# One softmax guard per head and image as the exp's bias operand, and small TensorE pieces in the even quads

## What is computed

```
h   = patches @ W + b + pos                              # 16 x 1024 x 64
xn  = ln(h)
q, k, v = xn @ Wq + bq, xn @ Wk + bk, xn @ Wv + bv       # 8 heads of 8
scores[b,h,i,j] = q_i . k_j / sqrt(8) + col_bias[h, j]   # 1024 x 1024 per head and image
out = softmax_j(scores) @ v
h   = h + out @ Wo + bo
h   = h + moe(ln(h))      # adds its own input too; experts w1, gelu, w2, 8 of them, top 2
```

## Time and profile before

| | us |
|---|---|
| median of 3 runs | 1176.74 (1175.11 to 1177.24) |
| the profiled execution | 1175.44 |
| its span, first to last instruction | 1173.6 |
| TensorE busy (share) | 1105.3 (94%) |
| ScalarE busy | 1030.7 (88%) |
| VectorE busy | 671.2 (57%) |
| GpSimd busy | 131.8 (11%) |

### The profile page before, as it was taken

One profiled execution on the slowest core, in us unless ns is written; L12 is line 12 of the kernel. 1 busy time (PEld: TensorE's weight loads), 2 busy tenths in 40 slices (PEclk: granted clock), 3 DMA queues, 4 the chain that ended last, 5 costly groups with the idle time before them and its releaser, 6 DMA issues. The chain is left out here.

```text
span 1173.6 us, 21907 instructions
## 1 busy us (share of the span) xinstructions
PE 1105.3 (94%) x7938; PEld 326.1 (28%) x7938; DVE 671.2 (57%) x1899; ACT 1030.7 (88%) x1127; POOL 131.8 (11%) x137
## 2 busy tenths in 40 slices
PE   3399999999999999999999999999999999899998
PEld 3122222222222222222222222222222222233332
DVE  9542756565656555565656565656565624367665
ACT  0199999999999999999999999999999999754553
POOL 4302201010101010101010101010101100000000
PEclk8589999999999999999999999999999999999999
DMA  2421323232323232323232323222222220022332
GB/s 52 111 74 39 85 53 82 53 83 53 83 53 84 53 83 53 83 49 87 49 88 49 86 50 73 63 68 67 62 67 55 72 61 10 16 63 66 84 75 50
DMA packets 63041, 75.93 MB, mean 65 GB/s; under 512 B 26338, under 2 KB 31458, under 8 KB 62906
## 3 DMA queue, kind: packets, MB, share of 16 engines
q1 hardware_dynamic: 60076, 73.01, 25.1%
q10 hardware_dynamic: 2350, 1.10, 0.4%
q0 software_dynamic: 480, 0.06, 0.1%
HBM read 37.54 MB, written 36.49 MB: 63 GB/s over the span
## 5 line engine op out<-in xcount | busy, mean ns | idle before, releaser
L1247 ACT ACTIVATE probs<-psum 128x1024 f32<-128x1024 f32 x1024 | 946.5, 1144 | 13.2 <-PE psum L1446 10.9
L1462 PE MATMUL psum<-probs,VA 128*32 128x512 f32 x4096 | 547.0, 606 | 5.3 <-DVE oT L1315 0.9
L1446 PE MATMUL psum<-QA,KA 54*128 54x512 bf16 x2048 | 331.7, 385 | 20.0 <-ACTq L1266 9.1
L1446 PEld LDWEIGHTS psum<-QA,KA 54*128 54x128 bf16 x2048 | 75.0, 93 | 491.5 <-ACT probs L1247 448.3
L1315 DVE STREAM_TRANSPOSE oT<-psum 128x512 f32<-128x512 f32 x64 | 45.9, 717 | 143.3 <-PE psum L1462 143.3
L1462 PEld LDWEIGHTS psum<-probs,VA 128*32 128x32 f32 x4096 | 82.1, 108 | 144.6 <-issue 86.1
L1282 ACT ACTIVATE probs<-psum,b 128x1024 f32<-128x1024 f32 x64 | 67.9, 1111 | 53.6 <-PE psum L1515 53.5
L1393 DVE TENSOR_TENSOR probs<-probs,psum 128x1024 f32<-128x1024 f32 x64 | 78.2, 1221 | 51.6 <-PE psum L1525 30.4
L484 DVE TENSOR_SCALAR qk<-psum,b_qk,scale_qk 128x512 f32<-128x512 f32 x32 | 25.8, 810 | 134.4 <-PE psum L673 134.4
L1515 PE MATMUL psum<-m_x,w 64*128 64x512 f32 x256 | 60.5, 591 | 1.5 <-ACT probs L1282 1.5
L1539 PE MATMUL psum<-probs,w 128*64 128x512 f32 x256 | 60.9, 598 | 0.0
(11 more groups left out here) (175 smaller groups left out, 830.9 us busy)
## 6 DMA issues: line engine op xcount, KB each, us to landing
QA<-q_parts_d SPq DMA_DIRECT2D x64, 192.0 KB
KA<-k_parts_d SPq DMA_DIRECT2D x64, 192.0 KB
q_parts_d<-qk_parts SPq DMA_DIRECT2D x31, 192.0 KB, 2.5
k_parts_d<-qk_parts SPq DMA_DIRECT2D x31, 192.0 KB, 2.7
xT<-in_xT SPq DMA_DIRECT2D x16, 256.0 KB, 2.6
x_d<-x2T SPq DMA_DIRECT2D x16, 256.0 KB, 2.1
m_x<-x_d SPq DMA_DIRECT2D x16, 256.0 KB, 2.7
out_h<-result SPq DMA_DIRECT2D x16, 256.0 KB, 3.2
```

The source lines that it names most:

```text
L1247: nc.scalar.activation(probs[:, k % PROB_BUFS, :], score_buf(buf_of(k)), ACT.Exp).then_inc(exped, 1)
L1446: last = pe.matmul(score_buf(buf_of(k))[:, (g % 2) * BANK:(g % 2 + 1) * BANK], KA[rows_of(h, SCORE_ROWS), h // 2, jt * P:(jt + 1) * P], QA ...
L1462: last = pe.matmul(o_acc[32 * g:32 * g + 32, :], VA[:, jt, h, :], probs[:, k % PROB_BUFS, (g % 2) * BANK:(g % 2 + 1) * BANK], start=(jt == ...
```

## The change

- The exp of a block gets a bias operand, `lift`, one value per partition: minus the larger bound of the block's two heads. `lift` is made once per image.
- The shift per query is gone, and with it `shift_of`, the DRAM tensor `shift_d` and `store_shift`. The three shift rows of `QA` stay (the fallback writes to them) and are loaded with zeros from SBUF.
- The largest key bias is taken off the bias rows in the prologue.
- A step `bound` takes the place of `flag`: TensorE spreads the 8 bounds to all partitions (ones times a diagonal), VectorE reduces them to `lift` and compares the largest with 31.
- `AUX_SLOTS`: nearly all pieces move to even slots (`bound` is in 15), and VectorE's own slots and `ROUTER_EXP_BLOCK` move along.
- On GpSimd `prep_rstd` of image b+2 moves ahead of `copy_v(0)`; in the prologue `prep_rq` moves ahead of `prep_rstd`.

The diff, cut to its core:

```diff
-AUX_SLOTS = {0: ("qk0", 0), 1: ("qk0", 1), 2: ("qk1", 0), 4: ("qk1", 1), 6: ("out_proj", 0), 7: ("out_proj", 1),
-             10: ("sq", 0), 13: ("post_t", 0), 16: ("router", 0), 18: ("router", 1), 19: ("flag", 0), 20: ("v", 0),
-             21: ("v", 1), 23: ("embed", 0), 24: ("embed", 1), 26: ("combine_t", 0), 29: ("norm_t", 0)}
+AUX_SLOTS = {0: ("qk0", 0), 2: ("qk0", 1), 4: ("qk1", 0), 6: ("qk1", 1), 8: ("out_proj", 0), 10: ("out_proj", 1),
+             12: ("sq", 0), 14: ("post_t", 0), 15: ("bound", 0), 16: ("router", 0), 18: ("router", 1), 20: ("embed", 0),
+             22: ("embed", 1), 24: ("v", 0), 26: ("v", 1), 28: ("combine_t", 0), 30: ("norm_t", 0)}
...
-CENTRE_SLOT, SCALE_SLOT, LEAD_SLOT, NORM_SLOT = 7, 9, 25, 27
-ROUTER_EXP_BLOCK = 38
+CENTRE_SLOT, SCALE_SLOT, LEAD_SLOT, NORM_SLOT = 10, 12, 23, 26
+ROUTER_EXP_BLOCK = 40
...
-COMBINE_SLOT, WEIGH_SLOT = 20, 22
+COMBINE_SLOT, WEIGH_SLOT = 20, 25
...
-                    rows = shift_d.rearrange("a (h t) i -> t a h i", t=2)
-                    sp.dma_start(QA[r, pairs, :], rows[par, :, pairs, :]).then_inc(aug_loaded[hg], 16)
+                    zeros = zeros3[:, :].bitcast(BF16).unsqueeze(1).broadcast_to([PARTS, 2, T])
+                    sp.dma_start(QA[r, pairs, :], zeros).then_inc(aug_loaded[hg], 16)
...
                 elif step == "sq":
-                    v.tensor_copy(sq[:, :], bank)
                     v.reduce_max(sq_max[:, :], bank, AX.X).then_inc(free, 1)
                     v.wait_ge(free, freed)
                     alone(v)
                     square_bounds(link)
-                    shift_of(bp, link, close)
+                    v.wait_ge(rq_ready, bp + 1)
+                    link(v.tensor_scalar(rq_clipped[:, :], rq[:, :], RQ_CLIP, None, ALU.min))
+                    close()
+                    v.tensor_scalar(rq_diag[:, :], ident[0:H, 0:H], rq_clipped[:, 0:1], None,
+                                    ALU.mult).then_inc(rq_spread, 1)
+                elif step == "bound":
+                    v.tensor_reduce(rq_top[:, :], bank[0:1, 0:H], AX.X, ALU.max)
+                    v.tensor_reduce(lift[:, bp % 2, :], bank[:, 0:H].rearrange("p (j t) -> p j t", t=2), AX.X, ALU.max,
+                                    negate=True).then_inc(free, 1)
                     v.wait_ge(free, freed)
...
+                    v.tensor_scalar(flags[0:1, ds(bp, 1)], rq_top[:, :], RQ_LIMIT, None,
+                                    ALU.is_gt).then_inc(flag_ready, 1)
...
+                elif step == "bound":
+                    pe.wait_ge(rq_spread, n + 1)
                     alone(pe)
-                    last = pe.matmul(aux[0:1, 0:1], excess[:, :], ones8[:, :], start=True, stop=True)
+                    last = pe.matmul(aux[:, 0:H], ones8[:, :], rq_diag[:, :], start=True, stop=True)
...
+                    sp.wait_ge(ones_ready, 2)
+                    load_shift(0)
+                    load_shift(1)
...
+                    v.memset(zeros3[:, :], 0.0).then_inc(ones_ready, 1)
...
-                    v.tensor_reduce(bias_top[:, :], bias_hj[:, :, :], AX.X, ALU.max).then_inc(bias_ready, 1)
+                    link(v.tensor_reduce(bias_top[:, :], bias_hj[:, :, :], AX.X, ALU.max))
+                    v.tensor_copy(bias_tops[:, :, :], bias_top[:, :].unsqueeze(2).broadcast_to([P, H, NCH])
+                                  ).then_inc(bias_ready, 1)
...
-                    link(v.tensor_copy(bparts[:, 0, :], biasT_bank))
-                    link(v.tensor_tensor(b_rest[:, :], biasT_bank, bparts[:, 0, :], ALU.subtract))
+                    link(v.reduce_max(bmax[:, :], top_bank, AX.X))
+                    link(v.tensor_scalar(bias_low[:, :], biasT_bank, bmax[:, 0:1], None, ALU.subtract))
+                    link(v.tensor_copy(bparts[:, 0, :], bias_low[:, :]))
+                    link(v.tensor_tensor(b_rest[:, :], bias_low[:, :], bparts[:, 0, :], ALU.subtract))
...
-                        store_shift(b + 1)
...
-                    nc.scalar.activation(probs[:, k % PROB_BUFS, :], score_buf(buf_of(k)),
-                                         ACT.Exp).then_inc(exped, 1)
+                    pair = 2 * (k // (BLOCKS // 2)) + k % 2
+                    nc.scalar.activation(probs[:, k % PROB_BUFS, :], score_buf(buf_of(k)), ACT.Exp,
+                                         bias=lift[:, b % 2, pair:pair + 1]).then_inc(exped, 1)
```

## The result

The changed kernel takes 1256.1 us (median of 4, 1255.4 to 1257.3) against 1176.3 us for the kernel before in the same comparison: a ratio of 1.068, 95% interval 1.066 to 1.070. That is 79.8 us more, where 84.3 were forecast. The profiled execution took 1255.38 us, with a span of 1253.4.

The account below looks back on a forecast made before the run. ScalarE was taken to bound the attention stage, TensorE close behind; 94.2 (operand) - 10.2 (small pieces) - 0.7 (image 0) + 1.0 (prologue) = +84.3 us on the 1176.74 us median, forecast 1261.0 us, range 1252 to 1275.

Parts of the forecast that it names:

- signs named: Expected in the changed profile: exp pitch 1.01 us, shortest exp 1.11, image 64.7 to 64.9, clock 1.00, first exp near 57.
- The bound: Attention stage: ScalarE paces it, busy 59.60 of 60 us, with TensorE close behind at 59.30.
- The operand: Attention exps: a per-partition bias adds 0.092 us to each of 1024, +94.2 us (92.2 to 96.3).
- The small pieces: Attention, pieces in even quads: TensorE always early, 0.73 us of gaps per image go, -10.2 us (-11 to -5).
- Image 0: First image at half clock: eight slower exps fill 0.7 us of ScalarE's idle time, -0.7 us (-2.8 to 0).
- The new wait: Slot 15, TensorE waiting for VectorE's diagonal: 9.4 us chain just hides in 9.45, cost 0, at most 5 us.
- The prologue: Before attention: VectorE's fill 0.5, bias-row steps +0.8, SP's removed store and reload -0.3; +1.0 us (-1 to +2).
- Rival A: Attention exps: operand read while the previous exp runs, exp stays 0.917 us, total 1169.7 us; 7 in 100.
- Rival C: Slot 15: chain to bound is late, TensorE stalls beyond its lead, 0.5 us per image, +8, 1269 us; 9 in 100.
- Rival B: Attention: TensorE's clock falls because it waits more in every quad, +45 us, 1306 us; 3 in 100.

Follow-up runs that it names:

- the run with other slots: Changed kernel without the exp's operand, out_proj in 6 and 8, sq 11, post_t 13, router 15 and 17, bound 18, weighing 23: 1210.0 us, ratio 1.028.

## Why the prediction was right

The forecast, 1261.0, was 4.9 us over the measured 1256.1, in the right direction and for the right cause. The small terms are partly right by luck: the prologue's error (+2.3 us) cancels those of image 0 (-1.1), of the gaps (-0.4 to -0.8) and of the expert stage (-0.4), and what is left is nearly the operand's alone. Two of the signs named did not come: an image takes 64.42 us and not 64.7 to 64.9, and the first exp starts at 59.5 and not near 57.

- **The bound.** ScalarE, with TensorE close behind: right. The operand in the kernel before alone gave 77.6 us.
- **The operand**, +94.2: the mechanism was right, the size 5% too large. It was taken from single durations (0.094) and pairs (0.090) of gelus; in a stream of 64 it is 0.0875 us, 89.6 in all, below the lower bound of 92.2. Two instructions behind an idle stretch are not yet a stream.
- **The small pieces**, -10.2: the gaps went, -10.6 to -11. But they went because of the slower exp, as the kernel before with the operand shows without one moved piece. The prediction's own sum (TensorE early in every pair of quads) said so; its heading gave the credit to the slots. It also had the images by one off: the full gaps are in images 0 to 13, image 14 has the first of them (0.23 us at block 44) and image 15 none, which changes the term little.
- **Image 0**, -0.7 forecast, -1.8 measured, inside its bounds. Most of it is not the change's. The second gap of the earlier trace rows, 0.90 us, is not in every execution of these instructions: the kernel before with an immediate bias has only the first,

```profile
63.91 12.02 ACT L1247 ACTIVATE probs<-psum 128x1024 f32<-128x1024 f32 x13 [1.88 <-PE psum L1446]
```

and its image 0 is 1.15 us shorter (61.50 against 62.65 us). The granted clock of TensorE is 0.99 from 64 us on there, while it is still 0.50 up to 66 us in the profile of the kernel before. Against that run the exps with an operand fill 0.5 us of the first gap in the kernel before (1.45 against 1.99 us lost at block 6, six exps of 0.0875 ahead of it), and 0.65 us in the changed kernel (1.05 and 0.29 lost). So the working, 0.7 us for eight exps, was about right, and the 1.8 us owe 1.15 to when the clock rises.
- **The new wait**, 0: right with the slow exp, but not by the working's margin. Its chain ended at the root, 9.4 us in 9.45. In the changed kernel it takes 9.14 us to the diagonal, and the copy of `post_t` behind it, which `bound` needs drained as well and which the sum leaves out, ends after 9.73 us (467.60 to 477.33). So it doesn't hide in 9.45 us: TensorE waits 0.4 us at `bound` in every image (4.9 us in twelve, for `x2T`), and another 0.4 at `combine_t` (5.2 us in twelve, for `v_new`). It is the lead of the score buffers, which the working named only as a reserve, that keeps both from ScalarE. With the exp at 0.917 us the five quads are shorter by 0.9 us, and the stalls reach it: 1.5 us per image from sq to bound and 0.84 at combine_t.
- **The prologue**, +1.0 forecast, +3.3 measured, above its bound of 2. The steps on VectorE were nearly right (1.3 us forecast, the store of the rows was issued 1.6 us later). What failed was to count -0.3 for SP's removed reload and nothing for the bias rows' own transfer: their store took 1.4 us longer than before, and the start followed ScalarE's reload of them with the reload of SP gone. The fill of the zero rows took 0.48 us on VectorE as expected.
- **Rival A** (the operand for free) was rightly improbable, but its time, 1169.7, was wrong: the run without the operand took 1197.7. The step that failed is "ScalarE needs 4 x 0.917 = 3.67 us for two quads where TensorE needs up to 3.71", which counts TensorE's work and leaves out the drains of the one bank that it waits for. Rival C was the larger missing part, and it belongs to a fast exp, not to the changed kernel; the stall at `combine_t` stands in no rival.
- **Rival B** (the clock) did not come about: 1.00 in the steady images. In the versions in which TensorE stands idle for about 1.5 us and more it does fall in many images.

## What to carry over

An operand per partition is paid by every ScalarE instruction, once for each operand and whatever the width, so on the bounding engine a shift that is the same for all is better folded into the matmul, an immediate, or left out where the range allows; on an engine with idle time it is free, as for the gelus here. A table of slots cannot be judged by the spacing of its pieces alone: where several steps share one bank, count for each step the time until the step before it is drained, with all that stands ahead of that drain in the other engine's queue. And test the parts of a change with the large one taken out: here the slower exp hid both a gap that the new slots were to close and a stall that they opened.

## What the runs showed of the hardware

- An ACTIVATE's bias costs nothing as an immediate (-4.0: ratio 1.000) and 0.089 to 0.092 us as a column, the same for 64 and for 1024 columns; a column for the scale adds another 0.092.
- I had not expected that so short an idle time could show in TensorE's clock, nor that it does not each time. In the run with other slots the same idle time of 1.59 us came in 14 images: in 8 of them the V matmuls behind it took 1.48 to 1.94 us, in the other 6 they took the 1.06 us of the full clock. In the changed kernel without the operand, idle times of 0.86 to 1.14 us (28 of them) were never followed by slower V matmuls. In the kernel before with the new slots, idle times of up to 3.7 us gave a mean clock of 0.90 over an image of 68.5 us. How much of the 9 us more is the standing and how much the clock after it was not separated.
- A 48 KB store to DRAM (the bias rows) was back, from its issue to the issue that waits for it, in 2.1 us ahead of the loads of the q and k rows and in 3.8 to 5.3 us among them.
